# Threshold search of a token-attention kernel: its column sums move to another PSUM bank, and its refinement to the head of the next slot

## The reference, cut to what matters

```python
# x: (32, 32, 110, 110) f32; K = 192 tokens, 8 heads, C = 32
y = conv(gn(x), conv_w, 7x7, dilation 5, padding 15) # one output channel
imp = sigmoid(gelu(batch_norm(y)))
xs = x * imp
idx = sort(top_k(imp.reshape(B, -1), K))             # the threshold search serves this
tokens = xs_tokens[idx] + positions[idx]
attn = softmax(q k^T / sqrt(4)); o = attn v          # per image and head
t1 = layernorm(tokens + o w_o); t2 = layernorm(t1 + mlp(t1))
xf = xs_or_x with rows idx set to t2                 # written back at idx
out = x + xf
```

## Time and profile before

| | |
|---|---|
| Median of 3 runs | 1444.02 us (1438.69 to 1449.96) |
| The profiled execution | 1437.04 us, of which its span 1435.1 us |
| PE busy | 1056.7 us, 74% |
| DVE busy | 1013.3 us, 71% |
| ACT busy | 678.6 us, 47% |
| POOL busy | 707.0 us, 49% |
| Mean granted clock of PE | 0.867 |

### The profile page before, as it was taken

The page is one execution under the profiler, slowest core; times in us unless marked ns, Lnnn a source line. Parts: engine busy times, 40 slices in busy tenths (PEclk is TensorE's granted clock), DMA queues, the critical chain, the costliest instruction groups (busy, mean ns, idle before and its releaser), DMA issues. The chain is left out here.

```text
span 1435.1 us, 25206 instructions
## 1 busy us (share of the span) xinstructions
PE 1056.7 (74%) x7976; PEld 838.0 (58%) x7976; DVE 1013.3 (71%) x2970; ACT 678.6 (47%) x1538; POOL 707.0 (49%) x957
## 2 busy tenths in 40 slices
PE   1596765687876897879777887789667768778656
PEld 1364544465755675668666766667456557566534
DVE  7345778677877788687878787878777776554533
ACT  1343232263534564546445654555355455557533
POOL 0221224542834476537654765468437745863353
PEclk8798888998998899899998998899979787989855
DMA  9498765754555788588965797555534525536558
GB/s 190 143 279 227 195 188 154 192 129 110 139 151 143 183 227 223 137 212 220 245 163 161 205 249 196 150 171 164 141 100 119 158 62 147 155 83 193 166 161 259
DMA packets 181239, 247.11 MB, mean 172 GB/s; under 512 B 70741, under 2 KB 77141, under 8 KB 181109
## 3 DMA queue, kind: packets, MB, share of 16 engines
q1 hardware_dynamic: 170613, 238.47, 61.2%
q10 hardware_dynamic: 2304, 4.65, 1.5%
q0 software_dynamic: 8192, 2.40, 1.1%
HBM read 123.62 MB, written 121.80 MB: 171 GB/s over the span
## 5 line engine op out<-in xcount | busy, mean ns | idle before, releaser
L860 ACT ACTIVATE pr<-sc,least 96x192 f32<-96x192 f32 x512 | 185.4, 413 | 341.7 <-DVE least L1244 341.0
L1001 POOL TENSOR_SCALAR res<-res,mom 128x440 f32<-128x440 f32 (+1 forms) x256 | 156.0, 611 | 366.5 <-DVE res L1289 361.3
L533 PE MATMUL cv<-X,w_conv 128*128 128x330 f32 (+1 forms) x1024 | 312.4, 431 | 10.8 <-ACT cvr L820 6.8
L651 PE MATMUL sc<-k_t,qm 128*96 128x192 f32 x1024 | 238.3, 360 | 24.4 <-ACT hid L892 7.5
L533 PEld LDWEIGHTS cv<-X,w_conv 128*128 128x128 f32 x1024 | 195.8, 207 | 53.6 <-ACT cvr L820 21.0
L834 ACT ACTIVATE wgt<-ib,eps_col,mom 128x440 f32<-128x440 f32 (+1 forms) x256 | 175.2, 691 | 106.9 <-PE ib L580 97.0
L1244 DVE TENSOR_REDUCE least<-sc 96x2 f32<-96x384 f32 x256 | 139.8, 549 | 117.4 <-PE sc L651 116.6
L812 ACT COPY xt<-xb 110x512 f32<-110x512 f32 x225 | 132.3, 588 | 166.9 <-PE xb L517 130.3
L517 PE MATMUL xb<-cst,X 128*110 128x128 f32 x900 | 155.2, 300 | 58.6 <-ACT xt L812 37.2
L651 PEld LDWEIGHTS sc<-k_t,qm 128*96 128x96 f32 x1024 | 170.9, 182 | 42.9 <-issue 29.6
L664 PE MATMUL pp<-cst,pr 96*96 96x96 f32 x1024 | 139.8, 262 | 54.6 <-ACT pt L871 51.9
(11 more groups left out here) (174 smaller groups left out, 1545.0 us busy)
## 6 DMA issues: line engine op xcount, KB each, us to landing
table<-xt SPq DMA_DIRECT2D x240, 224.0 KB
rt<-table SPq DMA_DIRECT2D x240, 224.0 KB
out<-res SPq DMA_DIRECT2D x320, 137.5 KB
X<-in_x SPq DMA_DIRECT2D x58, 412.5 KB, 5.5
X<-in_x SPq DMA_DIRECT2D x58, 343.8 KB, 4.3
conv_rows<-cvr SPq DMA_DIRECT2D x64, 188.0 KB
y<-conv_rows SPq DMA_DIRECT2D x64, 165.4 KB
out<-res SPq DMA_DIRECT2D x64, 68.8 KB
```

The source lines that it names most:

```text
L533: last = mm(cv[:, 0:CUT[half]], w_conv[:, 4 * q + z], X[:, m % XI, at0:at0 + CUT[half]], start=z == 0, stop=z == 3)
L651: last = mm(sc[0:HALF, k % 2, K * h:K * h + K], qm[:, 2 * pair + h, HALF * half:HALF * half + HALF], k_t[:], start=True, stop=True)
L860: last = A(pr[:, unit % 2, 2 * pair + h, :], sc[0:HALF, k % 2, K * h:K * h + K], ACT.Exp, scale=-1.0, bias=least[:, k % 2, h:h + 1])
L1001: last = gp.tensor_scalar(v, v, 1.0, mom[:, NB * g + b, 0:1], ALU.mult, ALU.add)
```

## The change

Two edits. The column sums, and with them the thresholds and offsets that are sent through PE, are written to bank `ib` in place of `tr`. The bookkeeping follows: a small matmul now waits for the `wgt_ok` of the last spread (list `weighed`), no longer for `res_ok`; the spread waits for the `small_rd` of the last small matmul, and the transposes back no longer do. And DVE runs `refine` of step k no longer behind the minima of its slot but first in the next slot, just in front of `count` of step k + 1; `find_first` moves with it.

```diff
@@ PE @@
-            searched, backed, backed_xb = [], [], []
+            searched, backed, backed_xb, weighed = [], [], [], []
             def count(g, k):
 
-                for value in backed[-1:]:
-                    pe.wait_ge(res_ok, value)
+                for value in weighed[-1:]:
+                    pe.wait_ge(wgt_ok, value)
                 pe.wait_ge(cnt_ok, upto(cnt_ok, g, k))
-                mm(tr[:, COUNT + k:COUNT + k + 1], blk[:], cnt[:], start=True, stop=True).then_inc(cnt_sum, 1)
+                mm(ib[:, COUNT + k:COUNT + k + 1], blk[:], cnt[:], start=True, stop=True).then_inc(cnt_sum, 1)
                 searched.append(upto(small_rd, g, k))
             def unit_back(g, u):
                 if bank is tr:
                     for value in backed[-1:]:
                         pe.wait_ge(res_ok, value)
-                    for value in searched[-1:]:
-                        pe.wait_ge(small_rd, value)
             def spread(g, u):
+                for value in searched[-1:]:
+                    pe.wait_ge(small_rd, value)
+                weighed.append(upto(wgt_ok, g, u))
                 mm(ib[:, 0:4 * H], bones[:], imp_b[:, at0:at0 + 4 * H], start=True, stop=True).then_inc(ib_ok, 1)
...
@@ thresholds and offsets of PE: the same two lines, tr -> ib, res_ok -> wgt_ok @@
...
@@ DVE @@
-                v.tensor_scalar(th[:, 1:2], tr[:, COUNT + k:COUNT + k + 1], K - 0.5, step, ALU.is_ge, ALU.mult).then_inc(small_rd, 1)
+                v.tensor_scalar(th[:, 1:2], ib[:, COUNT + k:COUNT + k + 1], K - 0.5, step, ALU.is_ge, ALU.mult).then_inc(small_rd, 1)
...
+                for g, n in at(s, SEARCH + 1, TOPK_STEPS):
+                    refine(g, n)
+                for g, n in at(s, MASKS):
+                    find_first(g)
                 for g, n in at(s, SEARCH, TOPK_STEPS):
                     count(g, n)
                 for g, n in at(s, BACK, U):
                     unit_back(g, n)
                 for g, n in at(s, SCORES, U):
                     for k in score_at.get(n, [])[0:2]:
                         least_of(g, k)
-                for g, n in at(s, SEARCH, TOPK_STEPS):
-                    refine(g, n)
...
-                for g, n in at(s, MASKS - 1):
-                    find_first(g)
                 for g, n in at(s, MASKS):
                     find_masks(g)
```

More of the change, by code:

```diff
@@ L582, in thresholds @@
             def thresholds(g):
-                for value in backed[-1:]:
-                    pe.wait_ge(res_ok, value)
+                for value in weighed[-1:]:
+                    pe.wait_ge(wgt_ok, value)
                 searched.append(upto(small_rd, g, TOPK_STEPS))
                 pe.wait_ge(tsel_ok, upto(tsel_ok, g))
-                mm(tr[0:H, THR:THR + NB], ones[:, 0:H], tsel[:], start=True, stop=True).then_inc(tb_ok, 1)
+                mm(ib[0:H, THR:THR + NB], ones[:, 0:H], tsel[:], start=True, stop=True).then_inc(tb_ok, 1)
             def offsets(g):
-                for value in backed[-1:]:
-                    pe.wait_ge(res_ok, value)
+                for value in weighed[-1:]:
+                    pe.wait_ge(wgt_ok, value)
                 searched.append(upto(small_rd, g))
                 pe.wait_ge(tot_ok, upto(tot_ok, g))
-                mm(tr[0:H, OFFS:OFFS + 8], tri, tot[:], start=True, stop=True)
-                mm(tr[0:H, TOTS:TOTS + 8], ones[0:H, 0:H], tot[:], start=True, stop=True).then_inc(off_ok, 1)
+                mm(ib[0:H, OFFS:OFFS + 8], tri, tot[:], start=True, stop=True)
+                mm(ib[0:H, TOTS:TOTS + 8], ones[0:H, 0:H], tot[:], start=True, stop=True).then_inc(off_ok, 1)
             def pick(g):
@@ L1109, in find_masks @@
                 dve.wait_ge(tb_ok, upto(tb_ok, g))
-                v.tensor_copy(tb[:], tr[0:H, THR:THR + NB]).then_inc(small_rd, 1)
+                v.tensor_copy(tb[:], ib[0:H, THR:THR + NB]).then_inc(small_rd, 1)
                 dve.wait_ge(small_rd, upto(small_rd, g, TOPK_STEPS))
@@ L1128, in find_ranks @@
                 dve.wait_ge(off_ok, upto(off_ok, g))
-                post(v.tensor_copy(off[:, 0:8], tr[0:H, OFFS:OFFS + 8]))
-                v.tensor_scalar(off[:, 8:12], tr[0:H, TOTS:TOTS + 4], -1.0, float(K), ALU.mult, ALU.add).then_inc(small_rd, 1)
+                post(v.tensor_copy(off[:, 0:8], ib[0:H, OFFS:OFFS + 8]))
+                v.tensor_scalar(off[:, 8:12], ib[0:H, TOTS:TOTS + 4], -1.0, float(K), ALU.mult, ALU.add).then_inc(small_rd, 1)
                 dve.wait_ge(small_rd, upto(small_rd, g))
```

## The result

The changed kernel takes 1504.99 us in the median of 4 runs (1504.47 to 1509.69), against 1441.7 us for the kernel before: a ratio of 1.045, 95% interval 1.042 to 1.049. That is +63 us where +30 was forecast. The direction was right; the size was not, and 1505 lies far up in the range of 1430 to 1512. The profiled execution took 1504.95 us, its span 1503.1 us, 68.0 more than before.

A forecast was written before the change was run, and what follows sets the result against it. PE and DVE were taken to bound the kernel by turns, a slot costing the maximum of the two. Terms -12 + 32 + 10 = +30 us, added to the median, gave 1474 us, range 1430 to 1512.

The forecast's parts named there:

- (b): Last five searches: column sum waits for ACT's weight of its own slot; +32 for four searches, +10 for the last.
- the walk of the fifth search: Fifth search, slot by slot: +6.6 us over nine slots with scores, -0.5 over eight without, +4 over the last seven.
- gives back what PE was late beyond DVE, -2: Masks, ranks and index behind a search: taken as DVE's alone, giving back PE's lateness, -2 us a period.
- (a): First three searches: DVE's tail no longer stands behind the column sum; -6.2, -4 and -2 us, sum -12.
- the last search: Eighth search: 3.6 us a slot against a chain of 4.1 in 16 slots with scores, +10 us.
- (c): PE's transposes back no longer wait for the refinement: worth nothing in the walk, bounds 0 and -21 us.
- (d): PE's spread waits for the refinement at the head of DVE's slot: hidden by (b), else up to 1 us a late slot.
- DVE's wait at the refinement: Sign in the profile after: DVE's waiting there for the column sum falls under 15 us in all, if (a) is right.
- The lower clock: PE's clock falling from 2.4 to 1.2 GHz after long waits: would raise the +32, given no term.
- Faster, by the decoupling alone: Rival: PE and DVE run ahead, so the weight is done when the sum is reached; 1406 or 1425 us, chance 0.13.
- Much slower: Rival: each wait for the weight undiminished, about 20 us a period, 25 for the last search; +93, 1537 us, chance 0.1.
- No change: Rival: DVE's tail absorbs the later sum, (b) shrinks to a third, 14 against -12; 1446 us, chance 0.22.

The follow-up runs named there:

- e3: Changed kernel with ACT making the weight before the first exponentials of the slot: 1427.1 us, ratio 0.991.
- e5: Kernel before with only ACT's weight put before the first exponentials: 1417.7 us, ratio 0.986.
- e4: Changed kernel with thresholds and offsets back in bank tr, column sums still in ib: 1492.8 us, ratio 1.038.
- e9: Kernel before with only thresholds and offsets sent through bank ib: 1502.8 us against 1485.0 on its chip, ratio 1.012.
- e8: e3 with the third search's refinement at its old place: 1418.9 us, ratio 0.986.
- e2: Kernel before with only the refinement moved first in the next slot, bank tr kept: 1483.2 us, ratio 1.029.
- e6: e1 with ACT's weight put before the first exponentials: 1431.0 us, ratio 0.994.
- e1: Changed kernel with refinement and find_first back at their old places, only the bank change kept: 1541.7 us, ratio 1.070.
- e10: Kernel before with weight before exponentials and, in the first two searches only, refinement first in the next slot: ratio 0.978 on the 1485.0 us chip.
- e11: e8 with thresholds and offsets back in bank tr: 1449.7 us against 1485.0 on its chip, ratio 0.976.

## Why the prediction was right or wrong

The mechanism was right: the wait for the weight behind the exponentials, confirmed by e3 with its control e5. The forecast's sum of +30 missed 38 of the 68 us of span, 37 of them in three terms.

**(b), the walk of the fifth search: right.** Nine slots with scores take 48.0 us where they took 42.2, +5.8 (6.6 forecast); the eight without, 32.5 against 33.3, -0.8 (-0.5); the last seven, 44.9 against 40.7, +4.2 (+4). Walking with durations from the trace worked, three times over.

**(b), "gives back what PE was late beyond DVE, -2": the step that failed.** The stretch of masks and ranks behind a search was called DVE's alone. It also holds small matmuls, the thresholds and above all the offsets, which the change sent to the new bank as well, and I didn't follow them there though I had listed them. The stretch grew by 4.6 us behind three searches and by 1.5 behind the seventh: +15.3 where -8 stood, a miss of 23 us. With the offsets back in `tr` (e4) the four stretches are still about 4 us longer than in the kernel before. So 11.5 us of the growth are the small matmuls' own, and the giving back didn't come even without them; why it didn't stays open. e9 prices the small matmuls' move alone at 17 us.

**(a), -12: too large.** The first search gave -7.0 (-6.2 walked) and was right. The second and third, for which I had put -4 and -2 without walking them, gave -0.4 and +4.0; in the third the late refinement costs, as the runs listed under e8 show. With start and gaps the early part is -3.8: 8 us short.

**(b), the last search, +10: it was +16.1.** I took the steps' mean against a bound of 4.1 us a slot; 24 steps of 4.3 came out. The 25 us that the rival took for this search undiminished were too many by 9. So more of the delay comes through here than I had, but not all of it; how much is absorbed was not tested. e3 brings the search to 86.7 us, so the cause is the same.

**(c)** was put at nothing. PE's 21.0 us before the transposes without a cause are gone from the changed kernel's waits, and no run takes this wait away alone; e2 shows how much it can grow with a late refinement when the bank is kept, 137.4 us of standing. **(d)** came as said, a wait of 36.6 us at the spread. What it costs once (b) is gone can be read from e3 against e6: up to 9 us over the last five searches.

**A sign that failed.** DVE's wait at the refinement was to fall under 15 us in all. It is 50.2 us where it was 51.5. In the first three searches (to 470 us) it fell from 20.0 to 11.6 us, but in the last five it rose from 31.6 to 38.6: the sum now comes so late that DVE stands for it even at the head of the next slot. Nor was ACT's order free in the kernel before, as I had written ("this kernel doesn't care"): e5 gains 21 us by changing it.

**The lower clock** got no term, because I wrote that my rows show the fall only behind the one long wait, and that "the new waits are of 1 to 2 us". The new waits reach 2.82 and 6.07 us, with a granted clock of 0.50 behind both. And the trace of the kernel before already had a fall behind a shorter wait. Behind the 2.39 us of the earlier trace rows the granted clock is 1.00 from 643 to 644 us and 0.50 from 644.5 to 646, and four scores take nearly twice the 0.81 us of the earlier trace rows:

```profile
645.49 1.48 PE L651 MATMUL sc<-k_t,qm 128*96 128x192 f32 x4
```

Over the whole span it matters little: the mean granted clock fell only from 0.867 to 0.861, and PE's busy time rose by 9.1 us, a small part of the 68. The Trainium skill (TensorE: Matmul & The Clock Gate, Part 1), which lets the array fall to half its clock when left idle, is borne out by the 0.50 behind both waits.

**The rivals.** "Faster, by the decoupling alone" named the point that decides it, whether the exponentials are over when the sum comes. They were not. e3 takes the weight out from behind them, and its ratio is 0.991. "Much slower" counted about 20 us a period undiminished; the searches showed 9 to 11, but e1, in which DVE too stands for the sum, came to +102 against that rival's +93. "No change" let DVE's tail absorb two thirds of (b) and kept 14 us of it; the last five searches alone grew by 55.

## What to carry to other kernels

Moving a buffer to another bank swaps one reader for another. Ask what stands in front of the new reader on its own in-order engine, and follow every instruction that goes along to the new bank, the rare ones too: the offsets, once in 30 slots, cost 11 to 17 us (e4, e9) where the five late searches with their 25 column sums each cost 55 together. If the new reader is late, move the reader: putting ACT's weight first took 78 us from the changed kernel. And try that reordering without the move, too: the old bank with it stands at 0.986, the new one with it at 0.991.

## What was not expected of the hardware

The kernel before takes about 1440 us on some chips and 1485 on another (9 runs, 1478.4 to 1487.7). On that chip the third search took 115.4 us in e9, 113.5 in e10 and 116.8 in e11, where it took 97.5 to 103.0 in all runs elsewhere. Against the profile before, this one search is 18 us longer in e9, while its fourth to seventh are within 3 us. Ratios to the kernel before on the same chip stayed usable. What differs in that stretch is not settled.
